# Choice of tokens: tiles normalized by VectorE and ScalarE, and now by GpSimd too

## What is computed

```python
logits = jnp.einsum('bsd,ed->bse', x, gate_w) + gate_b
probs = jax.nn.softmax(logits, axis=-2)
vals_t, idx_t = jax.lax.top_k(probs.transpose(0, 2, 1), K)
...
tok = jnp.take_along_axis(x, flat_idx[:, :, None], axis=1)
tok = tok.reshape(b, K, E, d)
merged = jnp.einsum('bked,bke->bed', tok, vals)
...
h = jax.nn.gelu(h, approximate=False)
...
out = jnp.zeros_like(x).at[jnp.arange(b)[:, None], flat_idx].add(out_tok)
```

## Time and profile before

| | us |
|---|---|
| median of 3 runs | 3369.23 |
| lowest and highest | 3367.02, 3377.65 |
| the profiled execution | 3362.04 |
| its span | 3360.3 |

### The profile page before, as it was taken

The page is one execution under the profiler, slowest core; times in us unless marked ns, Lnnn a source line. Parts: engine busy times, 40 slices in busy tenths (PEclk is TensorE's granted clock), DMA queues, the critical chain, the costliest instruction groups (busy, mean ns, idle before and its releaser), DMA issues. The chain is left out here.

```text
span 3360.3 us, 100843 instructions
## 1 busy us (share of the span) xinstructions
PE 2742.0 (82%) x45788; PEld 1544.8 (46%) x45788; DVE 1643.8 (49%) x2759; ACT 1434.0 (43%) x1417; POOL 799.0 (24%) x545
## 2 busy tenths in 40 slices
PE   2688788878788886688669999898999899998687
PEld 1355555555555565433334444444444444444333
DVE  3345444444444444520656666666666666663601
ACT  0444444444545443230135455555545455555511
POOL 3333333333434331000312222222211111211001
PEclk9688898889898886799679999999999999999898
DMA  6343424343433332469032222222212222220398
GB/s 177 90 103 89 103 73 103 77 105 81 115 86 97 87 88 63 155 256 408 14 85 56 55 58 58 58 58 58 57 40 56 50 58 50 57 58 2 151 421 333
DMA packets 265775, 351.89 MB, mean 105 GB/s; under 512 B 146938, under 2 KB 174404, under 8 KB 248964
## 3 DMA queue, kind: packets, MB, share of 16 engines
q1 hardware_dynamic: 235796, 314.46, 32.5%
q10 hardware_dynamic: 29552, 30.97, 3.8%
HBM read 274.26 MB, written 68.71 MB: 102 GB/s over the span
## 5 line engine op out<-in xcount | busy, mean ns | idle before, releaser
L1387 DVE TENSOR_REDUCE b_tops<-b_slot 128x8 f32<-128x1024 f32 x576 | 680.5, 1220 | 361.2 <-PE b_slot L1242 182.0
L1428 ACT ACTIVATE b_probs<-b_slot 128x1024 f32<-128x1024 f32 x576 | 582.7, 1022 | 552.5 <-PE b_slot L1242 396.4
L525 POOL COPY a_q_far<-a_q_near 96x1024 bf16<-96x1024 bf16 x128 | 258.5, 2049 | 336.1 <-PE a_slot L616 212.4
L1189 POOL TENSOR_SCALAR_AFFINE_SELECT b_probs<-b_probs 128x1024 f32<-128x1024 f32 x128 | 139.6, 1091 | 809.5 <-ACT b_probs L1428 809.5
L1262 PE MATMUL b_outT_ps<-b_probs,b_v 128*17 128x128 f32 (+3 forms) x4608 | 318.1, 384 | 6.1 <-ACT b_probs L1428 5.5
L1242 PE MATMUL b_slot<-b_q_stack,b_k_stack 99*128 99x512 bf16 (+3 forms) x1280 | 276.3, 323 | 43.3 <-DVE b_tops L1387 32.8
L913 ACT ACTIVATE a_k_far<-a_k_near 96x1024 bf16<-96x1024 bf16 x128 | 258.0, 2065 | 110.0 <-DMA a_k_near<-parts_near_dram 100.7
L1242 PE MATMUL b_slot<-b_k_stack,b_q_stack 96*128 96x512 bf16 (+3 forms) x1280 | 266.8, 323 | 29.6 <-DVE b_tops L1387 20.9
L813 DVE TENSOR_TENSOR a_probs<-a_slot,a_bias_k 128x1024 f32<-128x1024 f32 x128 | 154.1, 1217 | 184.1 <-PE a_slot L616 184.1
L822 DVE TENSOR_REDUCE a_tops<-a_slot 128x16 f32<-128x1024 f32 x128 | 156.2, 1221 | 137.5 <-PE a_slot L616 136.9
L876 ACT ACTIVATE a_probs<-a_probs 128x1024 f32<-128x1024 f32 x128 | 133.3, 1053 | 177.8 <-DVE a_probs L813 159.9
(11 more groups left out here) (228 smaller groups left out, 4271.4 us busy)
## 6 DMA issues: line engine op xcount, KB each, us to landing
f_w_ring<-in_L_ffn_w_dram SPq DMA_DIRECT2D x128, 1024.0 KB, 15.6
parts_near_dram<-a_parts ACTq DMA_DIRECT2D x96, 256.0 KB
parts_dram<-b_parts SPq DMA_DIRECT2D x96, 256.0 KB
a_k_near<-parts_near_dram SPq DMA_DIRECT2D x128, 128.0 KB, 3.0
b_k_stack<-parts_dram SPq DMA_DIRECT2D x64, 256.0 KB, 6.8
a_q_near<-parts_near_dram SPq DMA_DIRECT2D x64, 192.0 KB, 2.9
b_q_stack<-parts_dram SPq DMA_DIRECT2D x32, 384.0 KB, 4.4
values_dram<-a_v_stage SPq DMA_DIRECT2D x16, 544.0 KB, 3.7
```

Source lines behind the costliest of these rows:

```text
L525: pool.tensor_copy(q_far[far][0:QK_ROWS, h, :].rearrange("p (r a) -> p r a", r=LINKS), q_near[near][0:QK_ROWS, h, :].rearrange("p (a r) -> ...
L1189: pool.affine_select(out=blocks, in_=blocks, compare_op=ALU.is_ge, fill=0.0, base=0, pattern=[[0, NT], [1, P]], channel_multiplier=-1).the ...
L1387: ins = dve.tensor_reduce(out, src, AX.X, ALU.max)
L1428: act.activation(probs_of(b, g, u, h)[:, :], slot_of(step)[:, :], ACT.Exp).then_inc(taken_act, 1)
```

## The change

In both loops a quarter of the tiles is normalized by GpSimd, with the same operation (`tensor_scalar`, subtract and multiply, with the two numbers of each token read from SBUF). In the first loop it is the last tile of each chunk; VectorE has the other three. In the second, a pattern of eight tiles, "dadpdadp", gives four to VectorE (the even ones, as before), two to ScalarE and two to GpSimd. GpSimd's tiles wait for the same things as the others, and TensorE waits for them by a new semaphore, `z_ready_pool`. The choice of the second half stands after tiles 2, 6 and 10 on VectorE, after tile 5 on ScalarE, and ScalarE copies the turned weights after its tile 29. In f1 GpSimd's five steps on the rows of biases are put between its tiles of chunks 12 to 15, each behind a tile. To make room for the new semaphore, `exp_ready` and `wtok_ready` become one (`weights_taken`), `w_turned` and `merged_turned` another (`turned`), and `o_ready` joins `pre_ready`, each with counts to match.

```diff
@@ -1553,12 +1553,14 @@
...
-            z_ready_act = ssem("z_ready_act")
+            z_ready_act, z_ready_pool = ssem("z_ready_act"), ssem("z_ready_pool")
-            top_steps, exp_ready, w_ready, w_turned, wtok_ready = (
-                ssem(n) for n in ("top_steps", "exp_ready", "w_ready", "w_turned", "wtok_ready"))
-            merge_done, merged_ready, merged_turned = (ssem(n) for n in ("merge_done", "merged_ready", "merged_turned"))
+            top_steps, w_ready, turned, weights_taken = (ssem(n) for n in ("top_steps", "w_ready", "turned_back", "weights_taken"))
+            merge_done, merged_ready = (ssem(n) for n in ("merge_done", "merged_ready"))
+            exp_done, wtok_done, merged_turned = (1, 4), (3, 6), 5
...
+            Z_POOL = B * NT // 4
+            def z_again(n):
+                kind = "dadpdadp"[n % 8]
+                return kind, sum("dadpdadp"[m % 8] == kind for m in range(n + 1))
...
-                        pool.wait_ge(row_steps, 4)
                         pool.memset(dense["ones_rows"][:, :], 1.0)
-                        pool.wait_ge(rows_in, 32)
-                        for part in range(PARTS):
+                    def z_tile(n):
+                        t = tile_at(n)
+                        pool.tensor_scalar(zb[:, n % 8, :], x_sb[:, t, :], mv[:, t, 0:1], rstd[:, t:t + 1],
+                                           ALU.subtract, ALU.mult).then_inc(z_ready_pool, 1)
+                    def row_step(k):
+                        pool.wait_ge(row_steps, 4 + k)
+                        if not k:
+                            pool.wait_ge(rows_in, 32)
+                        part, rest = divmod(k, 2)
+                        if rest:
+                            pool.tensor_tensor(row[:, :, :], row[:, :, :], row_parts[:, part, :, :], ALU.subtract).then_inc(row_steps, 1)
+                        else:
                             pool.tensor_copy(row_parts[:, part, :, :], row[:, :, :]).then_inc(row_steps, 1)
-                            if part < PARTS - 1:
-                                pool.wait_ge(row_steps, 2 * part + 5)
-                                pool.tensor_tensor(row[:, :, :], row[:, :, :], row_parts[:, part, :, :], ALU.subtract).then_inc(row_steps, 1)
-                                pool.wait_ge(row_steps, 2 * part + 6)
+                    for c in range(CH):
+                        n = 4 * c + 3
+                        if n >= 8:
+                            pool.wait_ge(z_turned, n - 7)
+                        z_tile(n)
+                        if beside and c >= CH - 4:
+                            row_step(c - CH + 4)
+                    if beside:
+                        row_step(4)
+                    for n in range(B * NT):
+                        if z_again(n)[0] == "p":
+                            if n < 8:
+                                pool.wait_ge(z_turned, B * NT)
+                            else:
+                                pool.wait_ge(merge_done, n - 7)
+                            z_tile(n)
...
                             n = 4 * c + q
-                            pe.wait_ge(z_ready, n + 1)
+                            if q == 3:
+                                pe.wait_ge(z_ready_pool, c + 1)
+                            else:
+                                pe.wait_ge(z_ready, 3 * c + q + 1)
...
-                            pe.wait_ge(wtok_ready, 2)
+                            pe.wait_ge(weights_taken, wtok_done[0])
                         if n == B * NT // 2:
                             turn_weights(1)
-                            pe.wait_ge(wtok_ready, 4)
-                        if n % 2:
-                            pe.wait_ge(z_ready_act, n // 2 + 1)
+                            pe.wait_ge(weights_taken, wtok_done[1])
+                        by, nth_z = z_again(n)
+                        if by == "a":
+                            pe.wait_ge(z_ready_act, nth_z)
+                        elif by == "p":
+                            pe.wait_ge(z_ready_pool, Z_POOL + nth_z)
                         else:
-                            pe.wait_ge(z_ready, B * NT + n // 2 + 1)
+                            pe.wait_ge(z_ready, B * NT - Z_POOL + nth_z)
                         pe.matmul(bank[gq][32 * q:32 * q + NE, 0:D], wtok[:, i, gq, 32 * q:32 * q + NE],
                                   zb[:, n % 8, :], start=i == 0, stop=i == NT - 1).then_inc(merge_done, 1)
...
-                    for n in range(1, B * NT, 2):
+                    for n in [n for n in range(B * NT) if z_again(n)[0] == "a"]:
...
-                        if n == 11:
+                        if n == 5:
                             exponentials(1)
-                        if n == B * NT // 2 - 1:
+                        if n == B * NT // 2 - 3:
                             take_weights(1)
...
-                        for n in range(4 * c, 4 * c + 4):
+                        for n in range(4 * c, 4 * c + 3):
                             if n >= 8:
...
-                    for n in range(0, B * NT, 2):
+                    for n in [n for n in range(B * NT) if z_again(n)[0] == "d"]:
...
                         z_tile(n)
+                        if n == 2:
+                            top_max(1)
                         if n == 6:
-                            top_max(1)
-                        if n == 12:
                             top_mark(1)
-                        if n == 18:
+                        if n == 10:
                             top_weights(1)
```

More of the change, by code:

```diff
@@ L1639, in turn_weights @@
                                 ins = pe.transpose(bank[6 - 2 * gq + half][:, ii * P:(ii + 1) * P], wT[:, gq, i * P:(i + 1) * P], ident[:, :])
-                            ins.then_inc(w_turned, 1)
+                            ins.then_inc(turned, 1)
                     for c in range(CH):
@@ L1674, in _ @@
                             ins = pe.transpose(bank[2][:, (gq * KD + kd) * P:(gq * KD + kd + 1) * P], merged[:, gq, kd:D:KD], ident[:, :])
-                    ins.then_inc(merged_turned, 1)
+                    ins.then_inc(turned, 1)
                 @block.scalar
@@ L1681, in exponentials @@
                         act.activation(wT[:, gq, :], logits[:, gq, :], ACT.Exp, bias=neg_max[:, gq, :],
-                                       accum_out=total[:, gq, :]).then_inc(exp_ready, 1)
+                                       accum_out=total[:, gq, :]).then_inc(weights_taken, 1)
                     def take_weights(gq):
                         for half in range(2):
-                            act.wait_ge(w_turned, 2 * gq + half + 1)
+                            act.wait_ge(turned, 2 * gq + half + 1)
                             act.activation(wtok[:, 4 * half:4 * half + 4, gq, :],
-                                           bank[6 - 2 * gq + half][:, :].rearrange("p (i q) -> p i q", q=P), ACT.Copy).then_inc(wtok_ready, 1)
+                                           bank[6 - 2 * gq + half][:, :].rearrange("p (i q) -> p i q", q=P), ACT.Copy).then_inc(weights_taken, 1)
                     for c in range(CH):
@@ L1740, in top_weights @@
                     def top_weights(gq):
-                        dve.wait_ge(exp_ready, gq + 1)
+                        dve.wait_ge(weights_taken, exp_done[gq])
                         dve.wait_ge(top_steps, 5 * gq + 3)
@@ L1781, in _ @@
                         dve.tensor_scalar(dense["wqk"][:, 0, :, :, :], dense["wqk"][:, 0, :, :, :], HD ** -0.5, None, ALU.mult)
-                    dve.wait_ge(wtok_ready, 4)
+                    dve.wait_ge(weights_taken, wtok_done[1])
                     for n in (4, 5):
@@ L1790, in _ @@
                         dve.memset(bank[n][:, :], 0.0)
-                    dve.wait_ge(merged_turned, 1)
+                    dve.wait_ge(turned, merged_turned)
                     for gq in range(2):
@@ L1812, in ffn @@
                                   "hidT_ready", "out_done", "out_ready", "gathered"))
-            scattered, summed, o_ready, stored = (rsem(n) for n in ("scattered", "summed", "o_ready", "stored"))
+            scattered, summed, stored = (rsem(n) for n in ("scattered", "summed", "stored"))
             taken, added = rsem("taken"), rsem("added")
@@ L1936, in _ @@
                     gather(QUADS - 1)
-                    pe.wait_ge(o_ready, 1)
+                    pe.wait_ge(pre_ready, QUADS + 1)
                     for u in range(UNITS_OUT):
@@ L2020, in _ @@
                     dve.tensor_tensor(o_batch[:, :, :], bank[6][:, :].rearrange("p (g d) -> p g d", g=2),
-                                      b2[:, :].unsqueeze(1).to_broadcast([P, 2, D]), ALU.add).then_inc(o_ready, 1)
+                                      b2[:, :].unsqueeze(1).to_broadcast([P, 2, D]), ALU.add).then_inc(pre_ready, 1)
                     for u in range(UNITS_OUT):
```

## The result

| | before | after |
|---|---|---|
| median of 20 runs each, us | 3368.86 | 3379.80 |
| the profiled execution | 3362.04 | 3375.80 |
| its span | 3360.3 | 3374.0 |

The account below looks back on a forecast made before the run. VectorE was taken to bound the second loop's first half, ScalarE its second. f2: -0.40 + 1.37 - 1.65 = -0.68; f1: -1.03; total -1.7 from 3369.2 gives 3367.5 us, range 3360 to 3375.

Parts of the forecast that it names:

- What bounds the kernel: In the second loop, VectorE bounds the first half (busy 11.20 of 11.30 us), ScalarE the second (16 tiles in 7.96).
- GpSimd's tile: Both loops: one normalized tile on GpSimd takes 0.53 us, between a CAST's 0.396 and two passes at 0.79.
- The price of a meeting: VectorE tile overlapping a GpSimd tile loses 0.53 + 0.07 - 0.32 = 0.28 us; 24 meetings, 12 a stage.
- the long tile's rival: Both loops: GpSimd's tile at 1.34 us adds 19.4 us in meetings and 12 in chunks, giving 3399; chance 0.07.
- Half1's +1.37: Second loop's first half: meetings of GpSimd's tiles with VectorE's work add 0.25 + 4 x 0.28, in all +1.37 us.
- First loop: -0.40 in f2, -1.3 in f1: First loop: VectorE's fewer tiles save 0.40 us in f2; f1's row steps around chunk 13 save 1.3.
- meets nobody that matters: f1's first loop: GpSimd's tile 3 comes after its masks and delays nothing that matters, 0 us.
- Half2: -1.65: f2's second loop, second half: ScalarE's bound lifted, VectorE's copy starts at about +6.85 instead of +8.50, -1.65 us.
- Passed on one for one: After f2's choice: the experts' loads pass on whatever the choice gains or loses, one for one; nothing later absorbs it.
- The rival on the clock: TensorE's low-clock stretch after the idle 2.88 vanishes in both stages, up to 1.7 us each: 3364.1; chance 0.10.
- Rows late: f1: bias rows reach GpSimd late, delaying tiles 55 to 63; past about 1419 each us costs one; no chance given.

Follow-up runs that it names:

- e6: Changed kernel, no GpSimd in second loop; VectorE and ScalarE take 14 and 18 tiles of its first half, 20 and 12 of its second: 3355.39 us, ratio 0.998 to before.
- e9: e6's second-loop pattern with no GpSimd tile in the first loop either: 3358.56 us, ratio 0.9975 to the kernel before.
- e10: e6 run once more: 3356.28 us, ratio 0.9971 to the kernel before.
- e12: Changed kernel, but GpSimd's second-loop tiles go to a buffer nobody reads; VectorE and ScalarE make all 64: ratio 1.0008 to the kernel before.
- e4: Changed kernel with GpSimd's second-loop tiles written only 128 of 256 columns wide, part of the computation left out: ratio 1.0009 to the kernel before.
- e0: The bench: kernel before, plus GpSimd tiles timed with VectorE idle and VectorE bursts beside GpSimd work in f2's experts stage; 1236 ns a 256-column tile.
- e8: Changed kernel, GpSimd in first loop only; ScalarE takes three tiles of four in the second loop's second half: 3369.30 us, ratio 1.0011 to the kernel before.
- e5: Changed kernel without GpSimd in the second loop, VectorE and ScalarE alternating, the choice's steps kept at their early places: ratio 1.0011 to the kernel before.

## Why the prediction was wrong

**What bounds the kernel: right.** VectorE in half1 and ScalarE in half2 were the bounds; e6, e9 and e10 gained just there when tiles were moved off them.

**GpSimd's tile: the step that failed.** The prediction put it between a copy (0.396) and twice that (0.79) and took 0.53; it is 1.21 at least, 1.29 in the median. The nearest rows were a cast and a two-input operation, and the price was read between them. The bench shows what those rows could not: a copy 0.43, the two steps with constants 1.10, with two per-partition numbers 1.24. The upper price, 1.34, had been named, and given a chance of 0.07, although the only row against it was of another operation (0.669, two inputs). The forecast rested on 0.53, and with 0.53 a group of four is bound by VectorE; with 1.21 it is bound by GpSimd.

The estimates worked out from the Trainium skill's GPSIMD Engine Reference, sections 3 and 4.1, were 0.82 and 0.40 us; the trace agrees with neither. Against VectorE's 0.407 the tile is three times as long. The two sections don't disagree as the prediction had it: section 4.1 gives the factor of two for operations with two inputs.

**The price of a meeting: right in number, wrong in its working and in its count.** 0.28 us is what the bench measured. But it was worked out as GpSimd's length + 0.07 - 0.32, which for 1.30 would give 1.05; that the tile's error and the formula's cancel is luck. So the long tile's rival, 3399, was priced far too high: the formula put 24 meetings at full length and a further 12 us on the first loop, where the steady 1.60 us a chunk held. What decided was a mechanism that the prediction had nowhere for the second loop: one tile in four at 1.21 is longer than the 0.98 of four tiles before. Half1's +1.37 from meetings was 0.48 (e12). Beside GpSimd's tiles VectorE's search for the largest eight (1.22), its marking (1.20) and its first pass over the weights (1.20) lasted what they last without, only the second pass grew (0.93 against 0.75), and TensorE's own pace hides most of what the tiles behind them lose. Half2's meetings cost nothing.

The Trainium skill (SBUF — State Buffer, "SBUF: two separate sides") has the loser of the port blocked for the whole instruction. The runs agree nearly for a copy (0.72 of 1.10) and a subtraction (0.95 of 1.32), not for the tile (0.28 of 1.30).

**First loop: -0.40 in f2, -1.3 in f1.** The loop holds its 1.60 us a chunk, as forecast. f2 took 34.9, 35.6, 35.6 and 35.7 with VectorE alone and 33.9 to 36.9 (mean 35.2) with GpSimd, f1 38.2 to 39.4 (mean 38.6) against 36.1 to 39.6 (mean 37.9). Gains of 0.2 and 0.7 are of the forecast's sign and lost in the scatter. In f1 chunk 13, where GpSimd's bias steps hold VectorE up, gained as thought, and more: three tiles in 1.75 us, against 2.42 in the sum and four in 3.79 before. The tile behind the masks, "meets nobody that matters", did make TensorE's weight loads wait 0.94. Timelines of the kernel after, f1, VectorE's chunk 13 and TensorE's first chunk:

```profile
1422.36 1.75 DVE L1758 TENSOR_SCALAR f_zb<-x_sb,f_mv,f_rstd 128x256 f32<-128x256 f32 x3
...
1398.05 1.81 PEld L1685 LDWEIGHTS f_ps<-ident,f_zb 128*128 128x128 f32 x10 [0.94 <-POOL f_zb L1623]
```

**Half1: +1.37, measured +3.1 / +2.7.** Of it 0.48 are meetings and 0.67 the order of the steps, which was not in the sum at all; the rest is put down to GpSimd's pace (about 1.0) and the lower clock (0.6 to 0.9), neither of which was in the sum either.

**Half2: -1.65, measured +1.6 / +1.5.** The sign was lost with the tile's length. The relief of ScalarE is real, as e4 shows: 9.00 and 8.75 with GpSimd's instruction at 0.8 us.

**Passed on one for one: not quite.** The way to the first load grew by 0.5 and 2.5 as well, the clock there being 0.61 and 0.56, near the lower level of 1.2 GHz, instead of 0.79 and 1.00. The rival on the clock looked the other way, at a low stretch that might vanish.

**Rows late:** no. The bias rows reached GpSimd 25.2 us after f1's start, against 25.0 before.

## What to carry to other kernels

Before an engine gets a share of a loop, take a group of items, and compare the engine's time for its share of the group with what the group takes now: 1.21 us for one tile of four was over the 0.98 of four tiles, so the help set the pace, and with a ring of 8 buffers even one in eight did, since writing, merging and freeing its buffer took 2.15 against 1.96. Measure that one time where no row has the same instruction with the same kind of operands; a copy of the same size said a third of it. And look at idle time on the engines already in the loop first: moving four tiles in 32 from ScalarE to VectorE, and two the other way, gained what the change had been after.

## What the runs showed of the hardware

- GpSimd's tensor_scalar with two per-partition numbers, f32, 128 partitions: 0.59 us for 64 columns, 0.806 for 128, 1.24 for 256, 3.81 for 1024 with VectorE idle (e0), about 3.4 ns a column above 128; 1.21 at least and 1.29 in the median in the kernel after. With constants 1.10 for 256 columns, a copy 0.43; VectorE's takes 0.323 a tile in a row, 1.26 ns a column.
- GpSimd beside VectorE costs VectorE 0.28 us per such tile, 0.72 per copy of 1.10 and 0.95 per one-row subtraction of 1.32 (e0). GpSimd is stretched in turn: one of its tiles, beside VectorE's two passes over 128x1024 for the weights, took 2.83 (kernel after).
- TensorE's granted clock was below 1.00 in half1 or half2 of each choice in which TensorE waited for full GpSimd tiles, and 0.54 to 0.80 behind it in all eight; it stayed 1.00 in both halves where the same GpSimd work had no one waiting (e12), and where ScalarE set a slower pace (e8). The early order of the steps alone gave 0.86 in half1, in both choices (e5), and half-width GpSimd tiles with that order 0.62 and 0.74 (e4).
